# Every second group's segment sums turned by VectorE instead of TensorE, and the low parts of h0 made earlier, in a two-layer graph kernel

## The reference

```python
h = relu(layernorm(x))
# layer 0
msg = (h[src] + edge_attr) @ Wm.T + bm          # 40000 x 512
agg = segment_sum(msg, dst) / max(deg, 1)
u   = concat(h, agg) @ Wu.T + bu
o   = h + gelu(u)
x   = x + layernorm(o) * gamma + beta
# layer 1
h   = relu(layernorm(x))
rst = (1 + eps) * h + segment_sum(h[src], dst)
x   = x + relu(rst @ W1 + b1) @ W2 + b2 + h
```

## Time and profile before

| what | value |
|---|---|
| device time, three runs | 520.5 us median (518.84 to 520.79) |
| the profiled execution's own time | 520.12 us |
| its span (first to last instruction of the program) | 518.3 us |
| TensorE matmul busy | 481.5 us, 93% of the span, 3283 instructions |
| VectorE busy | 280.2 us, 54% |
| ScalarE busy / GpSimd busy | 147.3 us / 147.1 us, 28% each |
| the 79 groups, from the first to the last group's sums | 29.2 us to 269.8 us |
| of these the counting stage, groups 0 to 58 | 29.2 us to 200.6 us |

### The profile page before, as it was taken

One profiled execution on the slowest core, in us unless ns is written; L12 is line 12 of the kernel. 1 busy time (PEld: TensorE's weight loads), 2 busy tenths in 40 slices (PEclk: granted clock), 3 DMA queues, 4 the chain that ended last, 5 costly groups with the idle time before them and its releaser, 6 DMA issues.

```text
span 518.3 us, 9303 instructions
## 1 busy us (share of the span) xinstructions
PE 481.5 (93%) x3283; PEld 282.5 (55%) x3283; DVE 280.2 (54%) x612; ACT 147.3 (28%) x281; POOL 147.1 (28%) x197
## 2 busy tenths in 40 slices
PE   4789999998998998699999988999989999999997
PEld 3435555544544445477774755589944447644442
DVE  6897778877877879965734867973000000001111
ACT  4325532322222226413008444750012212100000
POOL 8332334433344437600000101237993000000000
PEclk9899999999999999889999998999999999999999
DMA  8997999999999999768930110131040000011111
GB/s 299 319 344 267 361 365 365 373 366 349 369 370 356 388 369 395 299 244 323 339 104 3 42 40 20 36 122 43 1 164 0 0 0 2 0 40 42 40 40 36
DMA packets 31115, 98.97 MB, mean 191 GB/s; under 512 B 3576, under 2 KB 3576, under 8 KB 31066
## 3 DMA queue, kind: packets, MB, share of 16 engines
q1 hardware_dynamic: 30458, 97.27, 51.5%
q10 hardware_dynamic: 608, 1.05, 0.7%
HBM read 95.76 MB, written 2.56 MB: 190 GB/s over the span
## 4 chain that ended last, share of the span: by engine, by line
PE 73%; DVE 16%; issue 6%; DVEq 2%; DMA 1%; ACT 1%; POOL 0%; SPq 0%; PEldq 0%; ACTq 0%; POOLq 0%
PE ps L1309 13%; PE ps L1294 13%; PE ps L1042 7%; PE ps L1089 7%; PE ps L1241 5%; PE ps L1061 4%; PE ps L1148 4%; DVE A L685 4%; PE ps L1149 4%; PE ps L1217 4%; PE ps L1218 4%; PE ps L1070 3%; PE ps L1050 3%; DVE stats L755 1%; DVE acc L722 1%
## 5 line engine op out<-in xcount | busy, mean ns | idle before, releaser
L414 POOL TENSOR_TENSOR aggT<-turned_sums,aggT 128x88 f32 x118 | 64.0, 542 | 101.2 <-ACT turned_sums L478 87.7
L685 DVE TENSOR_TENSOR A<-ps,A 128x220 f32 x158 | 60.7, 384 | 35.8 <-PE ps L1061 25.8
L979 DVE TENSOR_TENSOR U<-ps,U 128x512 f32<-128x512 f32 (+1 forms) x10 | 6.9, 691 | 130.5 <-PE ps L1309 130.5
L1294 PE MATMUL ps<-aggT,W1s 128*128 (+1 forms) x192 | 67.4, 513 | 1.9 <-PEq L1288 1.9
L1309 PE MATMUL ps<-W2s,hid 128*128 128x512 f32 (+1 forms) x160 | 68.8, 592 | 0.0
L1042 PE MATMUL ps<-ea,oneD 128*22 128x256 f32 x944 | 62.7, 383 | 0.1
L472 ACT COPY packed_sums<-ps 128x256 f32<-128x256 f32 x59 | 22.0, 372 | 113.6 <-PE ps L1042 113.5
L1294 PEld LDWEIGHTS ps<-aggT,W1s 128*128 128x128 f32 x192 | 36.4, 190 | 32.7 <-issue 32.7
L1061 PE MATMUL ps<-oneK,oneS 128*128 128x220 bf16 x316 | 42.1, 260 | 10.7 <-DVE A L685 10.3
L1309 PEld LDWEIGHTS ps<-W2s,hid 128*128 128x128 f32 (+1 forms) x160 | 30.0, 188 | 38.2 <-issue 38.2
L1217 PE MATMUL ps<-AR,Hh 128*128 128x256 f32 (+1 forms) x160 | 44.6, 314 | 3.9 <-DVE aggT L890 3.3
(11 more groups left out here) (142 smaller groups left out, 672.9 us busy)
## 6 DMA issues: line engine op xcount, KB each, us to landing
ea<-in_edge_attr_dram SPq DMA_DIRECT2D x78, 1024.0 KB, 7.5
X<-in_x_dram SPq DMA_DIRECT2D x1, 2304.0 KB
xt<-in_x_dram SPq DMA_DIRECT2D x9, 256.0 KB, 2.8
out_dram<-U SPq DMA_DIRECT2D x9, 256.0 KB
W1s<-in_L_gnn_W_dram SPq DMA_DIRECT2D x1, 2048.0 KB, 7.8
W2s<-in_L_gnn_W_dram SPq DMA_DIRECT2D x1, 2048.0 KB, 8.6
WuN<-in_L_gnn_Wu_dram ACTq DMA_DIRECT2D x1, 1024.0 KB, 5.3
WuN<-in_L_gnn_Wu_dram SPq DMA_DIRECT2D x1, 1024.0 KB, 6.8
```

The lines of the kernel that those rows point to most:

```text
L414: nc.gpsimd.tensor_tensor(cols, sums, cols, ALU.add).then_inc(early_step, 1)
L685: V.tensor_tensor(cols, ps[:, 4 + m % 2, half * KW:(half + 1) * KW].rearrange("p (h w) -> p h w", w=W), cols, ALU.add).then_inc(add_step, 1)
L1294: last = T.matmul(ps[:, CHUNK_BANK[k % 4], 0:cols], W1s[:, f, k * P:(k + 1) * P], aggT[:, f, bass.ds(start, cols)], start=f == 0, stop=f = ...
```

## The change

Two things are changed.

First, a list BLOCKS says for every group who turns it. Before, it was TensorE for n < 59 and VectorE after; now it is VectorE also for each odd n below 59. An odd group is summed in the form with 32 x 32 blocks; TensorE and ScalarE no longer turn and copy it; VectorE turns it at the head of its step n + 1, from PSUM into `turned_sums`; GpSimd adds it to aggT as before, out of the other layout, once it is turned. BY_BLOCKS and BY_TENSOR count the groups turned in either way up to n, and serve as the values that the semaphores are compared with. The sums of group n + 2 go into the same PSUM bank and now wait for that block transpose instead of ScalarE's copy.

Second, HH_AT is 34, 36, ..., 52 instead of 55 to 64: ScalarE makes the high part and GpSimd the low part of block b at step 34 + 2b.

```diff
@@ the lists of steps
-    HH_AT = [FULL - 3 + b for b in range(NT)]
+    HH_AT = [T_AT[-1] + 9 + 2 * b for b in range(NT)]
...
+    BLOCKS = [n >= EARLY or n % 2 == 1 for n in range(NG)]
+    BY_BLOCKS = list(itertools.accumulate(int(turns) for turns in BLOCKS))
+    BY_TENSOR = [n + 1 - turns for n, turns in enumerate(BY_BLOCKS)]
@@ GpSimd, add_sums_of
-                    if half == 0:
-                        pool.wait_ge(turned_out, n + 1)
+                    if half == 0 and BLOCKS[n]:
+                        pool.wait_ge(blocks_turned, BY_BLOCKS[n])
+                    elif half == 0:
+                        pool.wait_ge(turned_out, BY_TENSOR[n])
...
@@ ScalarE, the loop
-                if n < EARLY:
+                if not BLOCKS[n]:
                     packed_copy(n)
-                if 0 < n <= EARLY:
+                if n > 0 and not BLOCKS[n - 1]:
                     turned_copy(n - 1)
@@ VectorE, turn_blocks
                 dve.wait_ge(sums_done, n + 1)
-                if n < TURNS + EARLY:
+                if TURNS <= n < TURNS + EARLY:
                     dve.wait_ge(early_step, (n - TURNS + 1) * 2)
-                else:
+                elif n >= TURNS:
                     dve.wait_ge(sum_step, (n - TURNS + 1 - EARLY) * 2)
                 V.transpose(turned_sums[n % TURNS][:], ps[:, n % 2, 0:D // 2]).then_inc(blocks_turned, 1)
@@ VectorE, the loop
             for n in range(NG):
+                if n > 0 and BLOCKS[n - 1]:
+                    turn_blocks(n - 1)
                 if n > EARLY:
-                    turn_blocks(n - 1)
                     sum_first = offsets(n - 1)
@@ TensorE, sums
-                if 2 <= n < EARLY + 2:
-                    pe.wait_ge(packed_out, n - 1)
+                if n >= 2 and BLOCKS[n - 2]:
+                    pe.wait_ge(blocks_turned, BY_BLOCKS[n - 2])
                 elif n >= 2:
-                    pe.wait_ge(blocks_turned, n - 1 - EARLY)
-                if n < EARLY:
+                    pe.wait_ge(packed_out, BY_TENSOR[n - 2])
+                if not BLOCKS[n]:
...
```

More of the change, by code:

```diff
@@ L1 @@
+import itertools
 from contextlib import ExitStack
@@ L408, in add_sums_of @@
                     cols = aggT[:, :, bass.ds(first, W)]
-                    if half == 0:
-                        pool.wait_ge(turned_out, n + 1)
+                    if half == 0 and BLOCKS[n]:
+                        pool.wait_ge(blocks_turned, BY_BLOCKS[n])
+                    elif half == 0:
+                        pool.wait_ge(turned_out, BY_TENSOR[n])
                     if n > 0 or half > 0:
                         pool.wait_ge(early_step, n * 2 + half)
-                    sums = turned_sums[n % TURNS][:].rearrange("p (f q) -> p f q", f=FC)[:, :, half * QUAD:half * QUAD + W]
+                    if BLOCKS[n]:
+                        sums = turned_sums[n % TURNS][:].rearrange("p (h k w) -> p h k w", h=2, w=QUAD)[:, half, :, 0:W]
+                    else:
+                        sums = turned_sums[n % TURNS][:].rearrange("p (f q) -> p f q", f=FC)[:, :, half * QUAD:half * QUAD + W]
                     nc.gpsimd.tensor_tensor(cols, sums, cols, ALU.add).then_inc(early_step, 1)
@@ L469, in packed_copy @@
                 act.wait_ge(sums_done, n + 1)
-                if n >= TURNS:
-                    act.wait_ge(turned, n - TURNS + 1)
-                nc.scalar.copy(packed_sums[n % TURNS][:], ps[:, n % 2, 0:D // 2]).then_inc(packed_out, 1)
+                if BY_TENSOR[n] > TURNS:
+                    act.wait_ge(turned, BY_TENSOR[n] - TURNS)
+                nc.scalar.copy(packed_sums[BY_TENSOR[n] % TURNS][:], ps[:, n % 2, 0:D // 2]).then_inc(packed_out, 1)
             def turned_copy(n):
-                act.wait_ge(turned, n + 1)
+                act.wait_ge(turned, BY_TENSOR[n])
                 if n >= TURNS:
                     act.wait_ge(early_step, (n - TURNS + 1) * 2)
-                nc.scalar.copy(turned_sums[n % TURNS][:], ps[:, 2 + n % 2, 0:D // 2]).then_inc(turned_out, 1)
+                nc.scalar.copy(turned_sums[n % TURNS][:], ps[:, 2 + BY_TENSOR[n] % 2, 0:D // 2]).then_inc(turned_out, 1)
             def h0(b):
@@ L697, in add_sums_of @@
                 if half == 0:
-                    dve.wait_ge(blocks_turned, n + 1 - EARLY)
+                    dve.wait_ge(blocks_turned, BY_BLOCKS[n])
                 if n == EARLY and half == 0:
@@ L1065, in turn @@
             def turn(n):
-                pe.wait_ge(packed_out, n + 1)
-                if n >= 2:
-                    pe.wait_ge(turned_out, n - 1)
+                pe.wait_ge(packed_out, BY_TENSOR[n])
+                if BY_TENSOR[n] > 2:
+                    pe.wait_ge(turned_out, BY_TENSOR[n] - 2)
                 for c in range(2):
-                    last = T.transpose(ps[:, 2 + n % 2, c * P:(c + 1) * P], packed_sums[n % TURNS][:, c * P:(c + 1) * P], ident[:])
+                    last = T.transpose(ps[:, 2 + BY_TENSOR[n] % 2, c * P:(c + 1) * P], packed_sums[BY_TENSOR[n] % TURNS][:, c * P:(c + 1) * P], ident[:])
                 last.then_inc(turned, 1)
```

## The result

| | before | after |
|---|---|---|
| device time, median | 520.55 us (518.4 to 523.2, 20 runs) | 523.8 us (519.1 to 527.1, 20 runs) |
| ratio after / before | | 1.0044, 95% interval 1.0027 to 1.0061 |
| the profiled execution's own time, its span | 520.12, 518.3 us | 520.33, 518.5 us |
| sums of group 34 start | 133.38 us | 135.43 us (+2.05) |
| sums of group 53 start | 185.84 us | 194.01 us (+8.17) |

The change makes the kernel slower by 0.44%, 2.3 us by the ratio. The profiled execution of after is one of its quicker ones, and only 0.2 us longer than that of before. So the traces show where time moved; for what the change costs, the repeated runs count. Medians are of all runs of a kernel, while ratios leave out runs more than 1.5% above the kernel's fastest: one of the 20 of after, and four of the 12 of experiment three, whose ratio would be 1.0047 by the median of all.

What follows compares the result with a forecast made beforehand. In the counting stage TensorE and VectorE were taken to wait for each other in turn, TensorE slower by a tenth. Terms 1.8 + 4.9 - 6.85 = -0.15 us gave 520.0 us from 520.12, 80% range 515 to 525 us.

Steps and rivals of the forecast that it cites:

- Turns taken from TensorE: Even steps of the counting stage: 29 turns fewer, about 0.22 us saved each, 6.4 us if TensorE were always waited for.
- Transposes: VectorE in the counting stage: 29 block transposes added, 0.37 us each, 10.7 us in all; bounds 0 and 0.44 each.
- The new wait, and its places: Sums of group n + 2 wait for VectorE's transpose of n, 0.58 us from transpose to sums; to group 34 +1.8 us.
- From 34 to 53: Groups 34 to 53: +4.9 us, from +4.5 for ten low parts and +0.4 for the transposes; bounds -2 and +14.7.
- the +0.4 us for the transposes: Groups 34 to 53: the transposes' share of the +4.9 us forecast there.
- the layout: Step-by-step working from gaps between starts on TensorE and VectorE; group 34 to 43 without low parts: 25.3 us, before 25.1.
- Low parts beside VectorE: Steps 34 to 52: each low part on GpSimd costs VectorE between 0 and 1.1 us; +4.5 us for ten.
- From 53 to 63: End of the counting stage, without low parts: 25.6 us instead of 32.45, so -6.85 us; bounds -4.3 and -9.6.
- Sum: Whole kernel: 1.8 + 4.9 - 6.85 = -0.15 us, giving 520.0 us; group 63's shift is handed on to the end.
- Rival C: VectorE becomes the bound, +6.5 us in steps 34 to 53; in all +3.2 us, 523.3 us; chance 0.24.
- Rival A: Counting stage: low parts and transposes fall mostly in VectorE's waits; in all -5 us, 515 us; chance 0.29.
- Rival B: Counting stage: the turns taken from TensorE count in full; in all -9 us, 511 us; chance 0.05.

Runs made afterwards that it cites:

- experiment three: The changed kernel with low and high parts at the steps of u1's first halves (7, 12, ..., 52); 523.7 us, ratio 1.0026 to the kernel before.
- one: The changed kernel with the low parts back at their old steps, so the transposes alone; 531.4 us, ratio 1.0197 to the kernel before.
- two: The kernel before with only the low parts moved to steps 34 to 52, all turns on TensorE; 518.0 us, ratio 0.9938.
- eight: The changed kernel with two unused products on TensorE ahead of the sums of eight groups where it waits; 522.3 us, ratio 1.0025 to the kernel before.
- seven: The kernel before with 29 unused block transposes added on VectorE at the heads of even steps 2 to 58; 522.8 us, ratio 1.0044.
- five: The changed kernel with odd groups below 59 summed in two PSUM banks in turn, waiting for the transpose of n - 4; 516.3 us, ratio 0.9918.
- nine: The changed kernel with the transpose at the end of step n's additions, ahead of u1's addition; 521.6 us, ratio 0.9991 to the kernel before.
- ten: The changed kernel with the transpose within step n, between the table and the second half's addition; 521.5 us, ratio 1.0008 to the kernel before.

## Why the prediction was wrong

The forecast was no change; the kernel is slower by 0.44%, within the range given but on the side to which 0.24 was given.

- *Turns taken from TensorE.* Right: 1.00 us from sums to count after, forecast 1.04 between 1.00 and 1.10.
- *Transposes.* Right: the profile has 49 of 442 ns and 60 turns; the one-hot rows start 0.36 us behind one (155.50 to 155.86).
- *The new wait, and its places.* The mechanism and its price of 0.58 us from transpose to sums were right, and the waits came at 17, 21, 27, 41 and 57 as named, though also at 5, 11, 31, 47 and 51, and briefly at 35. To group 34 it made +2.05 (forecast +1.8).
- *From 34 to 53.* **This is the first step that failed:** the +0.4 us for the transposes. With nothing but the transposes in this stretch and a clock of 1.00 (one) it takes 54.85 us against 52.46 before, +2.4. The part that I laid out, from 34 to 43, came out nearly right: 25.55 against 25.27 us, +0.3, where the layout had 25.3 against 25.1. But then I carried the same rate on to 53, and from 43 to 53 it is +2.1 (29.30 against 27.19). The part laid out has one place where "all is lost again", the sums of 41; the part that was not has two, the sums of 47 and 51. The low parts have no share in these two waits, which are as long without them. The low parts' own +4.5 was nearly right, +4.7 alone (two). The two alone add up to 7.1 us and together they make +6.1, so that they do not make each other dearer here; the forecast had +4.9.
- *Low parts beside VectorE.* Right in kind: five one-hot operations took 0.65 to 1.31 us and three tables were 0.2 to 0.4 us too long between 135 and 195 us; eight were forecast. The size of 4.5 us agrees with 4.7 partly by luck, since 2.2 of these fell in a halved stretch that the layout did not have.
- *From 53 to 63.* 26.53 us against 25.6: right to 1 us, and the wait of 4.15 us is gone, as is the halved clock behind it. Ahead of the sums of 57 and 59 TensorE waits 1.67 and 1.01 us, where I had about 1.2 for both together.
- *Sum.* From the three terms the trace gives 2.05 + 6.12 - 5.92 = +2.25 us at group 63 where I had -0.15: 0.25 of the difference arose before group 34, 1.2 from 34 to 53, and 0.9 at the end of the stage. **Here is the second step that failed:** "from group 63 on TensorE [...] hands the shift on to the end" took the clock as given in both kernels. I had counted the fall that would go (near 215 us) and none that would come or go elsewhere. After has two in the counting stage, and before has one at 228.3 that after does not have, worth 2.0 us. So the profiled execution of after, 520.33 us, lies close to the forecast of 520.0 by luck. In the repeated runs: at a mean clock near 0.987 after takes 521.6 us (median of 5) and before 520.5 (24), at 0.98 524.0 (6) and 521.6 (19). So after is 1.1 to 2.4 us slower at one clock; and it is at 0.981 or lower in 11 of 19 runs, before in 20 of 71 (all runs of before beside the experiments). This is a comparison of groups of runs; that work in the waits takes the falls away is shown by eight, but not how much of the 2.3 us they cost.
- *Rival C* had the right sign and nearly the time (523.3), and its 6.5 us for the stretch from 34 to 53 is near the 6.12 measured, but its mechanism was another, VectorE out of time. Against that: in 133 to 186 us after VectorE was busy for 44.67 of 53 us; seven, with 45.29 us there, costs 2.3 us; and five, with the same instructions as the changed kernel and 47.67 us there, is faster than before. No time ran out; the order in which VectorE does things reached TensorE earlier.
- *Rival A* (VectorE hides it) is not what happened to the transposes; the gain it had comes with the second half of the change alone (518.0), and more so at the steps of u1 (514.0). *Rival B* is not borne out: freed of the wait, the change of the turns is worth nothing measurable. The figures of the Trainium skill that the prediction sets beside it, 390 and 311 ns, are for bf16; the tiles here are float32.

I named the wait, laid it out for one stretch of nine groups, and took its rate for the ten groups behind it. A layout of all 19 with both in place was the missing work.

## What to carry to other kernels

When work moves from one engine to another, look first at which buffer its result frees and who waits for that, then at the time of the instruction: here 0.27 us won per step was lost to a bank that came free behind other work on the new engine, at group 41 a table and two additions. One more bank returned 6.6 us; moving the instruction within VectorE's step returned 2.8 us at best (nine), and where it relaxed the wait ahead of sums most (ten) it lengthened the one ahead of counts. The Trainium skill asks for such banks (Perfetto Trace Analysis, Optimizing Tensor Performance: groups should rotate through different PSUM banks so that the emptying of one overlaps the next), and five agrees: two banks in turn were too few here, once VectorE emptied them. And a layout of a few steps holds for those steps: the same wait was worth 0.3 us in the nine groups that were laid out and 2.1 in the ten behind them. Work that blocks a neighbour belongs where the neighbour waits anyway: the same ten low parts cost 4.6 us up to group 53 at one list of steps (2.2 of it under half clock) and nothing at another.

## What the runs showed of the hardware

- TensorE's granted clock fell to half (0.50, 1.2 GHz) for 3.4 us at a time behind or within waits of 1.7 to 4.2 us (1.72 and 2.38 in after, 1.91 in two, 4.15 in before). Unused products in eight waits kept it at 1.00 from 133 to 186 us. Not every wait brings one: that of 1.05 us at group 21 did not, nor did any in one from 45 to 201 us, of up to 1.96 us.
- What a fall costs depends on where it falls: 2.2 us in step 42 of two, 2.0 us at 228.3 in before. Over the changed kernel's 19 runs the time rises by 3.6 us for each 0.01 that the mean clock is lower, so by that a fall of 3.4 us at half clock (0.0033 of the mean) costs some 1.2 us; over the 71 runs of before it is 2.1 us for 0.01. Both are estimates from how runs differ, in which other causes may go along with the clock.
- A block transpose of 128 x 256 in float32 takes 0.44 us from PSUM and lets the next instruction start after 0.36; a pair of TensorE transposes of the same data in a queue takes 0.27 us of it, less than VectorE needs.
- A low part on GpSimd (1.26 us where it starts ahead of VectorE's table or one-hot rows) is itself stretched to 1.72 and 2.10 us when VectorE's table was running first (at 140.30 and 170.94): each holds the other up, whichever is first. The additions to A16, which read PSUM, stayed at 0.37 to 0.39 us beside it.
